# A cross attention, head attention and expert layer on one core: the first tile, the order of loads and the order of the scores rearranged

## What is computed

```python
x = x + fake_quant(layernorm(x)) @ fake_quant(ctx)        # per batch; q = clip(round(v / s + z), 0, 255)
h = layernorm(x)
q, k, v = (h @ w.T + b for w, b in ((wq, bq), (wk, bk), (wv, bv)))   # 32 heads of 16 channels
# per token: 32 x 32 scores among its heads, softmax over the last axis, times v
x = x + softmax(q_heads @ k_heads.T / 4) @ v_heads
h = layernorm(x)
gate = softmax over the 16 largest of 64 router scores (h @ Wq_w.T @ keys.T)
x = x + 2 * ((h @ A_w.T) * gate per expert of 8 channels) @ B_w.T
```

## Time and profile before

| | us |
|---|---|
| median of the runs (3) | 146.35 |
| lowest to highest | 144.74 to 147.44 |
| profiled execution | 145.24 |
| its span in the profile | 143.2 |

### The profile page before, as it was taken

One profiled execution on the slowest core, in us unless ns is written; L12 is line 12 of the kernel. 1 busy time (PEld: TensorE's weight loads), 2 busy tenths in 40 slices (PEclk: granted clock), 3 DMA queues, 4 the chain that ended last, 5 costly groups with the idle time before them and its releaser, 6 DMA issues.

```text
span 143.2 us, 4290 instructions
## 1 busy us (share of the span) xinstructions
PE 118.7 (83%) x1860; PEld 70.1 (49%) x1860; DVE 96.8 (68%) x195; ACT 69.2 (48%) x88; POOL 47.5 (33%) x61
## 2 busy tenths in 40 slices
PE   0029559999597999895989999997999899899992
PEld 0023344455546538463555453963644367374881
DVE  5847975046987998695773167889245958995522
ACT  0366930997389994232847694328210124611120
POOL 3018204186727915722016787000207200002000
PEclk9999986999999999999999999999999999999999
DMA  2899999999999400059992100000001000000102
GB/s 58 304 416 419 387 432 390 409 398 387 413 426 389 181 5 0 5 199 389 370 422 96 73 7 0 5 5 0 5 16 60 0 5 5 0 5 0 73 0 73
DMA packets 7380, 24.43 MB, mean 171 GB/s; under 512 B 1217, under 2 KB 1473, under 8 KB 5698
## 3 DMA queue, kind: packets, MB, share of 16 engines
q1 hardware_dynamic: 7216, 24.16, 43.3%
q10 hardware_dynamic: 146, 0.01, 0.1%
HBM read 23.11 MB, written 1.05 MB: 169 GB/s over the span
## 4 chain that ended last, share of the span: by engine, by line
PE 55%; DVE 17%; ACT 8%; issue 7%; DMA 7%; POOL 3%; SPq 1%; DVEq 0%; ACTq 0%; POOLq 0%
PE ps_b L1173 18%; PE ps_a L1173 11%; DMA raw<-in_ctx_dram 7%; PE ps_att L1255 5%; ACT cu L467 3%; PE ps_att L1318 3%; DVE cu L687 3%; PE ps_att L1266 2%; PE ps L1108 2%; PE ps_t L1154 2%; PE ps_t L1127 2%; PE ps L1241 2%; DVE qT L794 1%; DVE eT L820 1%; ACT v_diag L493 1%
## 5 line engine op out<-in xcount | busy, mean ns | idle before, releaser
L374 POOL TENSOR_SCALAR cbf<-cu 128x2048 bf16<-128x2048 uint8 x13 | 24.9, 1923 | 15.9 <-ACT cu L467 9.7
L467 ACT ACTIVATE cu<-raw,sc_in,sc_recip 128x2048 uint8<-128x2048 f32 x13 | 26.9, 2090 | 3.0 <-DMA raw<-in_ctx_dram 2.9
L352 POOL TENSOR_SCALAR var_eps<-mean_var 128x1 f32<-128x1 f32 x11 | 3.0, 268 | 44.0 <-DVE mean_var L644 44.0
L1255 PE MATMUL ps_att<-kT,qT 16*32 16x32 f32 x1024 | 10.7, 193 | 3.9 <-issue 2.3
L1255 PEld LDWEIGHTS ps_att<-kT,qT 16*32 16x32 f32 x1024 | 9.6, 104 | 7.6 <-issue 7.5
L493 ACT COPY v_diag<-vT 32x512 f32<-32x512 f32 x16 | 10.1, 633 | 2.4 <-DVE vT L802 2.1
L642 DVE BATCH_NORM_STATS2 stats<-x_sb 128x6 f32<-128x512 f32 x12 | 8.1, 679 | 3.6 <-POOL x_sb L391 3.5
L1108 PE MATMUL ps<-q1T,cbf 128*128 128x33 bf16 x256 | 8.4, 178 | 2.6 <-DVE cbf L705 1.2
L1108 PEld LDWEIGHTS ps<-q1T,cbf 128*128 128x128 bf16 x256 | 7.6, 96 | 5.4 <-issue 2.3
L1085 PE MATMUL ps_t<-ident_bf,q 128*128 128x128 bf16 x16 | 1.8, 245 | 9.8 <-DVE q L672 9.8
L387 POOL TENSOR_TENSOR attn<-oT,o_recip 128x512 f32<-128x512 f32 x3 | 4.0, 1339 | 15.6 <-DVE o_recip L830 15.6
(11 more groups left out here) (148 smaller groups left out, 236.1 us busy)
## 6 DMA issues: line engine op xcount, KB each, us to landing
raw<-in_ctx_dram SPq DMA_DIRECT2D x13, 1024.0 KB, 10.6
raw<-in_ctx_dram SPq DMA_DIRECT2D x6, 512.0 KB, 11.3
wq<-in_L_attn_wq_dram SPq DMA_DIRECT2D x1, 1024.0 KB, 13.6
wk<-in_L_attn_wk_dram SPq DMA_DIRECT2D x1, 1024.0 KB, 13.4
wv<-in_L_attn_wv_dram SPq DMA_DIRECT2D x1, 1024.0 KB, 15.7
wa<-in_L_ffn_A_w_dram SPq DMA_DIRECT2D x1, 1024.0 KB, 12.8
wb<-in_L_ffn_B_w_dram SPq DMA_DIRECT2D x1, 1024.0 KB, 11.0
out_dram<-x_sb SPq DMA_DIRECT2D x3, 256.0 KB, 2.0
```

What stands on the lines that cost most here:

```text
L374: nc.gpsimd.tensor_scalar(cbf[:, n % BF_SLOTS, :, :], cu8[:, n % U8_SLOTS, :], -CENTER, 1.0, ALU.add, ALU.mult).then_inc(sem_ctx_bf_pool, 1)
L467: nc.scalar.activation(cu8[:, n % U8_SLOTS, :], raw[:, n % RAW_SLOTS, :], ACT.Identity, bias=sc_in[:, 3:4], scale=sc_recip[:, 2:3]).then_i ...
L1255: last = nc.tensor.matmul(ps_att[Q * j:Q * j + H, i, :], qT[rows, i, :], kT[rows, i, :], start=True, stop=True)
```

## The change

Seven parts. (1) Contexts 1 and 2 are loaded in halves as well; ACT quantises the first half of 1 and all of 2, DVE the second half of 1; DVE quantises x tile 0 in ACT's place. (2) The router's weights and keys are loaded ahead of Wq, and transposed and combined on PE during tile 0, in front of `transpose_h2(0)`, into another bank. (3) The filler is 3+2+3 matmuls of 128 columns at three places instead of 3 of 512 at one; `keep_clock_up(5)` is gone. (4) Context 7 goes ahead of Wv, and SP waits for the first part of tile 0's scores before it issues contexts 8 to 11 and Wa. (5) `scores` takes a range of tokens, and each part is issued in two calls; for tile 1 halves of `project_v` and the y1 transposes stand between them. (6) Tile 0's scores come right behind `project_k(0)`, ahead of tile 1's products, and `project_v(0)` behind the scores. (7) The lists of ACT, DVE and PE are reordered to go with it, in later tiles too.

```diff
-        halved = (BPT - 1, 2 * BPT - 1)
+        halved = (1, BPT - 2, BPT - 1, 2 * BPT - 1)
         def quantised(n):
-            if n == BPT - 2:
-                return (sem_ctx_u8_vector, 2)
-            return (sem_ctx_u8, n + 1 - (n > BPT - 2))
+            if n == 1:
+                return (sem_half_u8, 1), (sem_ctx_u8_vector, 1)
+            return ((sem_ctx_u8, n + 1 - (n > 1)),)
...
             load_x(1, 2, sem_x1_in)
+            sp.dma_start(wr[:, :, :], chunked(wrT)).then_inc(sem_router_in, 16)
+            sp.dma_start(keys[:, :], keysT).then_inc(sem_router_in, 16)
             sp.dma_start(wq[:, :, :], chunked(wqT)).then_inc(sem_wq_in, 16)
             load_ctx(4)
             load_ctx(5)
             sp.dma_start(wk[:, :, :], chunked(wkT)).then_inc(sem_wk_in, 16)
             load_ctx(6)
+            load_ctx(7)
             sp.dma_start(wv[:, :, :], chunked(wvT)).then_inc(sem_wv_in, 16)
-            load_ctx(7)
             load_x(2, 4, sem_x_rest_in)
-            sp.dma_start(wr[:, :, :], chunked(wrT)).then_inc(sem_router_in, 16)
-            sp.dma_start(keys[:, :], keysT).then_inc(sem_router_in, 16)
+            sp.wait_ge(sem_scores_done, 1)
             load_ctx(8)
...
-            quantise_x(0)
+            act.wait_ge(sem_recip, 1)
             quantise_ctx(0)
             quantise_ctx(1)
+            quantise_ctx(2)
             quantise_ctx(3)
...
             shift_x(0)
+            copy_router_rows()
+            copy_router_weights()
             copy_first_h2T()
             quantise_ctx(4)
             quantise_x(1)
             quantise_ctx(5)
+            quantise_ctx(6)
             copy_q1T(1)
+            quantise_ctx(7)
             shift_x(1)
-            quantise_ctx(6)
-            quantise_ctx(7)
+            quantise_x(2)
             quantise_ctx(8)
-            copy_router_rows()
-            quantise_x(2)
             quantise_ctx(9)
+            exp_scores(0, 0)
             copy_h2T(1)
-            copy_router_weights()
+            exp_scores(0, 1)
             quantise_ctx(10)
-            exp_scores(0, 0)
-            exp_scores(0, 1)
+            quantise_ctx(11)
             copy_q1T(2)
+            quantise_x(3)
             place_v(0)
-            quantise_ctx(11)
-            quantise_x(3)
...
+            quantise_first_x()
             center_q1(0)
             row_sum_term(0)
             copy_q1T(0)
             turn_identity()
-            quantise_ctx(2)
+            quantise_ctx_half(1)
...
             bias_q(0)
+            spread_heads(qT, q_sb, sem_q_biased, sem_qT_ready, 0)
             bias_k(0)
-            spread_heads(qT, q_sb, sem_q_biased, sem_qT_ready, 0)
             spread_heads(kT, k_sb, sem_k_biased, sem_kT_ready, 0)
             dve.wait_ge(sem_x_rest_in, 16)
             norm_stats(x_sb[:, 2, :], 0, 2, sem_ln1_stats, sem_ln1_mean)
+            softmax_shift(0, 0)
+            norm_1(2)
+            finish_product(1)
+            softmax_shift(0, 1)
             norm_stats(x_sb[:, 3, :], 0, 3, sem_ln1_stats, sem_ln1_mean)
-            finish_product(1)
-            norm_1(2)
             residual_1(1)
+            center_q1(2)
             norm_2_stats(1)
             norm_1(3)
             norm_2(1)
-            center_q1(2)
+            transpose_probs(0, 0)
             bias_v(0)
-            softmax_shift(0, 0)
-            softmax_shift(0, 1)
+            transpose_probs(0, 1)
             transpose_v(0)
-            transpose_probs(0, 0)
-            transpose_probs(0, 1)
...
-                    nc.tensor.matmul(ps_att[:, S:, :].rearrange("p i h -> p (i h)"), ones[:, :], bias_rows[:, 0:D],
+                    nc.tensor.matmul(ps_att[:, S:S + P // H, :].rearrange("p i h -> p (i h)"), ones[:, :], ones[:, :],
...
             product(0, 2, 3)
+            keep_busy(3)
             product(0, 3, 4)
+            transpose_router_weights()
             transpose_y1(0)
+            keep_busy(2)
+            combine_router_weights()
             keep_busy(3)
             transpose_h2(0)
...
             project_k(0, second)
+            scores(0, 0, early)
+            scores(0, 0, late)
             product(1, 0, 1)
-            project_v(0, first)
             product(1, 1, 2)
             product(1, 2, 3)
-            scores(0, 0)
             product(1, 3, 4)
-            transpose_router_weights()
+            scores(0, 1, early)
+            scores(0, 1, late)
             transpose_y1(1)
+            project_v(0, first)
             project_v(0, second)
-            combine_router_weights()
             transpose_h2(1)
-            scores(0, 1)
...
             project_k(1, second)
+            product(2, 0, 1)
             context(0)
-            product(2, 0, 1)
             product(2, 1, 2)
             product(2, 2, 3)
             product(2, 3, 4)
+            scores(1, 0, early)
             project_v(1, first)
-            scores(1, 0)
+            scores(1, 0, late)
+            scores(1, 1, early)
             transpose_y1(2)
             project_v(1, second)
-            scores(1, 1)
+            scores(1, 1, late)
...
-            keep_clock_up(5)
```

More of the change, by code:

```diff
@@ L365, in center_ctx @@
                                             ALU.add, ALU.mult).then_inc(sem_half_bf_pool, 1)
-                    pool.wait_ge(*quantised(n))
+                    for landed in quantised(n):
+                        pool.wait_ge(*landed)
                     pool.wait_ge(sem_half_bf_pool, 1)
@@ L701, in center_ctx @@
                     return
-                dve.wait_ge(*quantised(n))
+                for landed in quantised(n):
+                    dve.wait_ge(*landed)
                 if n >= BF_SLOTS:
@@ L1054, in _ @@
             gates(2)
+            sum_gates(2)
             gate_z(2)
-            sum_gates(2)
             t = TILES - 1
@@ L1243, in router_scores, with scores @@
                 last.then_inc(sem_router_done, 1)
-            def scores(t, part):
-                if part == 0:
+            def scores(t, part, tokens=range(S)):
+                if part == 0 and tokens[0] == 0:
                     pe.wait_ge(sem_qT_ready, t + 1)
                     pe.wait_ge(sem_kT_ready, t + 1)
+                    if t == 0:
+                        pe.wait_ge(sem_wr_keys, 1)
                     if t >= 1:
                         pe.wait_ge(sem_oT_ready, t)
-                for i in range(S * part, S * (part + 1)):
+                for i in range(S * part + tokens[0], S * part + tokens[-1] + 1):
                     for j in range(BPT):
@@ L1326, in _ @@
             first, second = range(0, KC // 2), range(KC // 2, KC)
+            early, late = range(0, S // 2), range(S // 2, S)
             transpose_q1(0)
@@ L1385, in _ @@
             project_v(2, second)
-            scores(2, 0)
+            product(3, 0, 1)
+            transpose_h3(1)
             product(3, 1, 2)
-            transpose_h3(1)
             product(3, 2, 3)
+            scores(2, 0, early)
+            scores(2, 0, late)
             product(3, 3, 4)
@@ L1392, in _ @@
             bottleneck(1, first)
-            scores(2, 1)
+            scores(2, 1, early)
+            scores(2, 1, late)
             transpose_y1(3)
@@ L1406, in _ @@
             transpose_h3(2)
-            scores(3, 0)
+            scores(3, 0, early)
+            scores(3, 0, late)
             project_v(3, second)
             router_scores(2)
-            scores(3, 1)
+            scores(3, 1, early)
+            scores(3, 1, late)
             bottleneck(2, first)
```

110 lines of the change are left out of this document (56 added, 54 removed).

## The result

The changed kernel takes 146.94 us (median of 15 runs, 145.5 to 149.34) against 145.27 for the kernel before in the same session (15 runs, 143.85 to 148.94). The ratio is 1.0123, interval [1.0079, 1.0167]: slower by 1.2%, where a change of -0.1% was forecast. That is clear of 1.0, but less than the 2% that the forecast took as the least that can be told. The profiled execution is 146.94 us with a span of 144.0; before it was 145.24 with 143.2. So 0.8 us came in inside the span and 0.9 outside it.

The account below looks back on a forecast made before the run. Loads and an ACT/DVE chain bound the start, PE the middle and end, then a tail. Terms +0.6-0.3-0.45 = -0.15 us, from the runs' median 146.35, gave 146.2 us (chance 0.40), 8-in-10 range 141.3 to 149.5.

Parts of the forecast that it names:

- the sum at the end: Whole kernel: output(0) lag, part of it vanishing, and tail gain add to -0.15 us, span 143.2 to 143.05.
- the 2.04 us around the span: Time of the profiled execution outside its span, carried over unchanged: 145.24 us becomes 145.1 us.
- Part 1: First tile: project_q(0) begins at 23.3 us instead of 25.66, a gain of 2.35 us, with no clock loss taken.
- Part 2: Up to tile 0's scores: Wk lands about 27.0, kT ready at 33.7, first scores at 33.75, 4.1 us earlier.
- Part 3: Hand-over to tile 1: late x tiles and DVE's order put project_q(1) at 48.2 us, context(0) 3.1 us late.
- Part 4: From context(0) to the end: delay shrinks to 0.25 us at h3 transposes; late Wb delays output(0) by 0.6.
- I let 0.3 of the 0.6 disappear in waits such as 98.55: After output(0): 0.3 us of its 0.6 us delay is absorbed in later waits.
- So 0.45 counts: Tail: removing five filler matmuls lets output(2) start 0.65 us earlier, of which 0.45 us is gained.
- R1: Gain kept, PE bounds from 23.3 us on: start 2.35, router 1.7, tail 0.45 all won; 141.85 us, chance 0.28.
- R2: Slower: place_v(0) behind contexts 10 and 11 on ACT holds context(0), 2.25 us gaps return; 149.5 us, chance 0.20.
- R3: Reordering does nothing because loads pace both kernels; only the tail counts; 145.9 us, chance 0.06.
- R4: Clock stays at 1.2 GHz through project_q(0), making kT up to 3.4 us later; 146.7 us, chance 0.06.

Follow-up runs that it names:

- e2: Kernel before with its three filler matmuls ahead of transpose_h2(0) cut from 512 to 128 columns; ratio 0.9966.
- a1: Changed kernel without SP's wait for the first part of tile 0's scores before contexts 8 to 11 and Wa; 148.56 us, ratio 1.0199.
- a2: Changed kernel with Wb issued right behind Wa, ahead of contexts 12 and 13; 145.19 us, ratio 0.9994.
- a4: Changed kernel with the five tail filler matmuls back ahead of output(2); 145.79 us, ratio 1.0107.
- c1: Changed kernel with three filler matmuls of 512 columns (six records) ahead of the first scores; 148.18 us, ratio 1.0204.
- c4: Changed kernel with Wb behind Wa, DVE's hand-over order of the kernel before, and ACT's copy_h2T(1) and place_v(0) moved ahead of contexts 9 and 11; 147.43 us, ratio 1.0151.
- d1: Changed kernel with Wb right behind Wa and the five tail filler matmuls back; 144.67 us, ratio 1.0019.
- after_again: The changed kernel run again, unaltered, against the kernel before; 146.28 us, ratio 1.0072.
- a3: Changed kernel with twelve filler matmuls of 128 columns ahead of the first scores; 157.54 us, ratio 1.0818.
- c2: Changed kernel with tile 1's scores issued whole again instead of in quarters; 145.55 us, ratio 1.0116.
- c3: Changed first tile and load order without the held loads, then the kernel before's ACT, DVE and PE lists; 149.42 us, ratio 1.0286.
- e1: Changed kernel with Wb behind Wa and ten one-column bf16 matmuls, five ahead of context(3), five ahead of output(2); 144.11 us, ratio 0.9992.
- d2: Kernel before with Wb issued right behind Wa, ahead of the wait for tile 1's scores and contexts 12 and 13; 146.23 us, ratio 1.0071.

## Why the prediction was wrong

The forecast's chain of times held to within 0.7 us up to output(0), but for Wk, kT and the first scores (1.0 to 1.1 late) and context 9 (1.3 late). The middle of it, where both the gain and its loss were expected, was right. The step that failed is the sum at the end, +0.6-0.3-0.45 = -0.15 us, and the 2.04 us around the span that it carried over. Inside the span it came to +0.8 us, and 0.9 came in around it.

- **Part 1** held: project_q(0) at 23.25 (forecast 23.3), granted clock 1.0 in 20 to 24 us. That the clock was worth a worry is seen in e2, where thin filler without the router work around it leaves the projection at 6.05 us in the profiled execution, 2.35 more than before. The Trainium skill ("TensorE: Matmul & The Clock Gate", the section on why this matters for kernels) advises against idle gaps of PE in mid-kernel. e2 agrees in direction: it had four gaps, each of only 0.7 to 1.0 us, from 16 to 24 us, and the low clock with them. In the changed kernel none of the 3.4 us that the forecast put at this place came.
- **Part 2**: Wk landed at 28.1, not 27.0. I had kept its 13.4 us from issue to landing; it took 14.7. The router's transfers ahead of it aren't the reason: a1, a2, a4, c1, c4 and d1 have them too and 13.4 or 13.5 us, while after_again, a3, c2, c3 and e1 have 14.5 to 14.9. What makes the difference isn't known. kT and the first scores are 1.1 late for it (34.83 against 33.75). On DVE it cost nothing, since DVE waited for x until 37.17 anyway; on SP it held back contexts 8 to 11, which wait for these scores. The idle time of 2.95 us was forecast at 2.8, its effect on the clock was not: I looked for the low clock at project_q(0) and it came at 35 to 45 us. At project_q(1) no cost of it can be told (c1 against a2, a4 and d1).
- **Part 3** held in the sum: x landed at 37.15 (bounds 36.05 and 37.25, taken 36.6, so the upper bound was right), DVE's chain took 9.86 us (10.05 in the text, though its terms add up to 10.09), context 9 landed 1.3 later than forecast (45.66 against 44.4) because the held contexts were issued 1.7 later (36.76 against 35.1), project_q(1) came at 48.80 (48.2; bounds 47.8 to 48.6), context(0) at 56.99 (57.0).
- **Part 4**, up to output(0), held: h3 transposes 66.37 (66.5), Wb landed at 74.8 (74.75), output(0) +0.74 (+0.6). a2 shows that Wb is the whole of this lag. Its size varies between executions: in the profile of after_again Wb was issued at 63.84, landed at 73.94, and output(0) began at 74.06, level with before. The reason given for the missing gaps was wrong: c2 has them gone without the quarters, which is what the forecast's sentence on the page about refills had said of splitting. The gaps stand at a fixed count of instructions (345 in a1, a3, c1, c4 and d1, whatever code is there), so an edit ahead of them moves other code into their place.
- **The sum failed** in three terms. "I let 0.3 of the 0.6 disappear in waits such as 98.55" had no row for it, and nothing disappeared: the lag was 0.80 at context(3), 50 us later. "So 0.45 counts" for the tail filler: it was 0.26 to 0.29. And a term was missing: context(3), unchanged in code, took 1.47 us instead of 1.16. It did so in a4, which has the filler, too, so it isn't the filler's absence; e1's ticks in front of it took it away. Inside the span: +0.80+0.31-0.28 = +0.83, measured +0.8.
- **The span and what lies around it.** I carried 2.04 us over unchanged. It became 2.94 in the profiled execution, by medians 0.8 more, for a packet of instructions behind the last of them. a4, d1 and e1 show that it comes ahead of the end, and the extra time is gone, with ten more PE records, whatever these do, and c1 that six aren't enough (2.65 to 3.04 us around the span). It is at least half of the measured loss (0.9 of 1.7 us in the profiled executions; 0.8 by the medians of the first set, whose times differ by 1.0), and the forecast had it at nothing without a reason.
- **The rivals.** R1 needed the gain kept to the end; but x landed at 37.15, not by 34.5, and between 28 and 57 us PE waited 0.81, 2.95, 0.84 and 0.66 us for others. R2 had its mechanism (context(0) at 57 behind ACT) but not its price: with no gaps in tile 1, PE, with one product less behind context(0), caught up 3.0 of 3.1 us. Had the gaps of 2.26 us come back there, the 146.94 us would have been about 149.2, an estimate, near its 149.5. R3 counted the tail's 0.45 alone and missed by the same terms as the forecast. R4 was a drop at the wrong place.
- The Trainium skill ("Runtime: NRT & Kernel Launch", Instruction fetch mechanics) calls the cost of the refills mostly hidden. Most of the 14 or 15 packets here leave no gap; some that meet a run of short matmuls or full load queues do, up to 5.88 us in a3.

No version here beats the kernel before by more than can be told. The best are the changed kernel with Wb behind Wa and ten ticks (e1: 144.11, 0.9992 [0.9954, 1.0031]) and d1; both take back the change's loss, and both spread less in their 12 runs (1.8 and 0.8 us from lowest to highest) than the kernel before beside them (3.7 in 23 runs and 4.2 in 29).

## What to carry to other kernels

Add to every estimate the places where the instruction packets fall: look for the packets of the instruction queue, see which "issue" gaps end just after one, and count the PE records ahead of the gap. Take it as a thing that stays at its count while an edit moves the code, not as a property of the code around it. A transfer that is needed late but issued behind a wait (Wb here, 1.1 us) is the cheapest thing to look for after a reordering. An early start is worth what the next wait leaves of it; write down which landing or chain sets the next hand-over before counting it.

## What the runs showed of the hardware

- A fetch of instructions starts late beside bulk loads. Gaps on PE end 1.2 to 1.6 us after a q8 packet ends; the long ones stood beside loads (2.83 us in a1, 2.80 in c3, 5.88 in a3), those late in the kernel, with few loads, were 0.6 to 2.0 (c1, a3). With one line of SP's list taken out (a1) the packet started 4.7 us behind the first scores instead of 1.7. The packets' own length says less: 0.9 us at 43.0 of the changed kernel, with 421 GB/s around it, and 1.35 us at 126.75 with hardly any load. The whole of it is inferred from times and counts; no row names the fetch as a releaser.
- The gaps stand at fixed counts of instructions: behind 345 PE records in five kernels, behind 345 and 473 in a3 and behind 725 and 853 in the kernel before, so 128 matmuls, each with its weight load, apart. The count is fixed, the time of a packet isn't: the first packet of a4 came at 30.5 us, that of the changed kernel at 23.25, with the same lists up to the tail.
- The last packet can come behind the last instruction, and then 0.7 to 0.8 us more lie around the span. It has no row among the instructions and no share in the span. This goes with the kernel in all 16 profiled ones, but three runs of two kernels with such a packet in their profile (two of after_again, one of a2) have 1.89 to 1.97 us.
- The same PE list with the same 1.62 us of idle time on PE had the granted clock at 2.4 GHz behind it in one execution (before) and at 1.2 GHz in another (d2), and 1.5 us between them at project_q(1). After the 2.95 us of idle time ahead of the first scores it fell in every profile of the changed kernel and of the variants that keep it.
- The stall behind the first matmul of context(3) stands at the count of 1737 at which c1 has a gap after a packet, so it is likely the crossing into a newly fetched piece of code. That isn't shown: in the changed kernel the packet before it fell at 120.5 and had ended 4 us earlier, so nothing was left to wait for.
